# Four kinds of attention in one kernel: the sums of a wide step in a ring of four PSUM banks, and a query's low part first

## The reference, cut to what matters

```
q, k, v = x @ Wq, ctx @ Wk, ctx @ Wv          # layers 0, 2: heads of 64
logits  = q k^T * scale + col_bias            # -20 * (1 - mask) on chosen keys
x       = softmax(logits) @ v @ Wo + bo + x
xn      = x * rsqrt(mean(x*x) + eps) * norm_w # layers 1, 3: heads of 16
x       = x + softmax(q k^T * scale) @ v @ wo
```

## Time and profile before

| | |
|---|---|
| median of 3 runs | 1754.18 us (1751.69 to 1755.21) |
| the profiled execution's own time | 1748.67 us |
| its span (first to last instruction) | 1746.9 us |
| PE / DVE / ACT / POOL busy | 93% / 69% / 59% / 27% of the span |
| chain that ended last | PE 46%, issue 16%, DVE 10%, POOL 7%, ACT 3% |
| granted TensorE clock, mean | 0.968 |

### The profile page before, as it was taken

The page is one execution under the profiler, slowest core; times in us unless marked ns, Lnnn a source line. Parts: engine busy times, 40 slices in busy tenths (PEclk is TensorE's granted clock), DMA queues, the critical chain, the costliest instruction groups (busy, mean ns, idle before and its releaser), DMA issues.

```text
span 1746.9 us, 29686 instructions
## 1 busy us (share of the span) xinstructions
PE 1617.9 (93%) x10732; PEld 882.6 (51%) x10732; DVE 1197.9 (69%) x2313; ACT 1023.9 (59%) x1737; POOL 471.9 (27%) x353
## 2 busy tenths in 40 slices
PE   7998698999999999999999999899999999999794
PEld 6886444444545454544545454445454545454442
DVE  5474547676777687768777777678777877775551
ACT  2111165666667676767666766576676767676452
POOL 5342402123222231223131313132322322232212
PEclk9898898999999999999999999999999999999986
DMA  7998402151315121512353323412151325131422
GB/s 255 323 317 242 140 25 58 37 98 28 84 32 132 27 78 27 131 35 80 69 115 91 73 54 80 91 40 72 41 122 27 82 41 125 26 81 23 123 69 81
DMA packets 176738, 160.57 MB, mean 92 GB/s; under 512 B 91722, under 2 KB 133066, under 8 KB 175570
## 3 DMA queue, kind: packets, MB, share of 16 engines
q1 hardware_dynamic: 174578, 150.29, 33.5%
q10 hardware_dynamic: 2016, 8.39, 1.2%
HBM read 115.11 MB, written 43.48 MB: 91 GB/s over the span
## 4 chain that ended last, share of the span: by engine, by line
PE 46%; issue 16%; DVE 10%; POOL 7%; ACT 3%; SPq 3%; DMA 3%; POOLq 0%; ACTq 0%; DVEq 0%
PE general L1649 9%; PE general L1528 7%; POOL kept L1402 4%; PE score_ps L1587 4%; PE score_ps L1588 4%; PE out_ps L1605 4%; PE general L1545 3%; PE general L1549 3%; PE score_ps L1576 2%; PE out_ps L1625 2%; DVE q_pair L1440 2%; DVE q_aux L1439 2%; SPq L1135 2%; DVE q_pair L1441 2%; PE general L1669 2%
## 5 line engine op out<-in xcount | busy, mean ns | idle before, releaser
L1451 DVE TENSOR_REDUCE tops<-general 128x2 bf16<-128x308 f32 x1024 | 433.2, 470 | 88.1 <-PE general L1545 40.1
L1292 ACT ACTIVATE probs<-score_ps 128x512 f32<-128x512 f32 x512 | 297.7, 598 | 141.0 <-PE score_ps L1588 128.0
L1402 POOL TENSOR_TENSOR kept<-kept,inv_b 128x512 f32<-128x512 f32 x128 | 170.7, 1355 | 464.9 <-DMA inv_b<-scratch_inverses 464.9
L1438 DVE CAST q_aux<-q_pair 64x512 bf16<-64x512 f32 x160 | 74.8, 468 | 194.1 <-ACT q_pair L1280 192.9
L1304 ACT ACTIVATE q_aux<-general 4x512 bf16<-4x512 bf16 x320 | 187.5, 586 | 31.7 <-PE general L1558 26.1
L1279 ACT ACTIVATE q_pair<-general 64x512 fp32r<-64x512 f32 x160 | 94.6, 591 | 156.7 <-PE general L1528 156.1
L1545 PE MATMUL general<-w_top,q_aux 128*128 128x154 bf16 x1024 | 133.4, 237 | 36.5 <-DVE q_pair L1441 26.1
L1341 ACT ACTIVATE a_hi<-kept 128x512 fp32r<-128x512 f32 x160 | 93.6, 624 | 112.0 <-POOL kept L1402 48.1
L1464 DVE TENSOR_TENSOR a_lo<-kept,a_hi 128x512 fp32r<-128x512 f32 x160 | 123.9, 807 | 49.7 <-ACT a_hi L1341 48.9
L1392 POOL TENSOR_TENSOR x_lo<-xn,x_hi 128x1024 fp32r<-128x1024 f32 x31 | 73.6, 2375 | 285.0 <-ACT x_hi L1260 145.6
L1588 PE MATMUL score_ps<-q_pair,w_pair 128*128 128x512 f32 x256 | 149.4, 589 | 0.0
(11 more groups left out here) (157 smaller groups left out, 3305.7 us busy)
## 6 DMA issues: line engine op xcount, KB each, us to landing
inv_b<-scratch_inverses SPq DMA_DIRECT2D x128, 256.0 KB, 4.8
w_pair<-scratch_wk_hi SPq DMA_DIRECT2D x32, 256.0 KB, 4.9
x<-scratch_stream SPq DMA_DIRECT2D x16, 512.0 KB, 3.3
inv_n<-scratch_inverses SPq DMA_DIRECT2D x256, 32.0 KB, 1.9
xn<-scratch_stream SPq DMA_DIRECT2D x15, 512.0 KB, 3.4
scratch_stream<-x SPq DMA_DIRECT2D x14, 512.0 KB, 4.9
scratch_wk_hi<-p_kout_hi SPq DMA_DIRECT2D x16, 308.0 KB
p_raw<-in_L_xattn_Wk_dram SPq DMA_DIRECT2D x4, 1024.0 KB, 7.8
```

The lines of the kernel that those rows point to most:

```text
L1292: nc.scalar.activation(dst, score_ps[:, number % 2, :], ACT.Exp, scale=scale).then_inc(act_exp.sem, 1)
L1402: last = nc.gpsimd.tensor_tensor(tiles[i], tiles[i], (inv_b, inv_n)[n % 2][:, i, :], ALU.mult)
L1451: last = nc.vector.tensor_reduce(tops[:, n % 2, sub, 2 * pair:2 * pair + 2], src, AX_X, ALU.max)
```

## The change

1. `GB` is 4. sum_ps is gone; value n 1 of a wide step takes a bank of the ring for its sums, with `start=True` at every step. DVE takes the bank: at the first step of a chunk as a copy to wide_sums, at the three others as an addition to it. ACT's copy and PE's wait for it are gone.
2. DVE does a query's two subtractions before its two casts.
3. `ORDER`, `FIRST` and `LAST` are new throughout. In `FIRST` query 8 0 and 8 1 come in step 2.
4. At the start of the layers POOL, not DVE, clears the first half of q_aux, and ACT, not SP, issues the DMAs of w_top's key rows and of the first mask rows.
5. In `prepare` both layers' norm weights are loaded behind the second piece of weights.

```
-        normw = sb("p_normw", [P, KC])
+        normw = sb("p_normw", [P, 2, KC])
...
                 load_piece(1)
+                for p in range(2):
+                    sp.dma_start(normw[:, p, :], ins[f"L{2 * p + 1}_xattn_norm_w"].rearrange("(k p) -> p k", p=P)).then_inc(s_nw, 16)
...
-GB = 3
+GB = 4
...
-GENERAL = [(*x, m) for x in PLAN if x[1] in ("query", "max", "turn", "output", "square", "rate", "give")
+WIDE_STEPS = [n for n in range(STEPS) if wide(n)]
+GENERAL = [(*x, m) for x in PLAN if x[1] == "value" and x[2] in WIDE_STEPS and x[3] == 1 or x[1] in ("query", "max", "turn", "output", "square", "rate", "give")
...
-        sum_ps = ctx.enter_context(nc.psum_tensor("sum_ps", [P, 512], F32))
...
-        reader = {"query": dve_query, "max": dve_max, "turn": act_turn, "output": dve_output,
+        reader = {"value": dve_sums, "query": dve_query, "max": dve_max, "turn": act_turn, "output": dve_output,
...
         def _(act):
+            act.wait_ge(rows_cleared, 1)
+            load_top_rows(act, 0)
+            act.wait_ge(first_cleared, 1)
+            load_masks(act, 0)
...
-                elif what == "sums":
-
-                    if n % 2 == 0:
-                        wait(act, pe_value.sem, pe_value.after(it, "value", 4 * n + 3, 1))
-                        wait(act, sums_stored.sem, sums_stored.after(it - (n == 0), what, 2 - n, 0))
-                        nc.scalar.activation(wide_sums[:], sum_ps[:], ACT.Copy).then_inc(act_sums.sem, 1)
...
         def _(pool):
+            nc.gpsimd.memset(q_aux[:, 0].bitcast(F32), 0.0).then_inc(first_cleared, 1)
...
-            for buf in (w_top[:], q_aux[:, 0], w_aux[:], w_aux_rest[:], tops[:]):
+            for buf in (w_top[:], w_aux[:], w_aux_rest[:], tops[:]):
...
-                    nc.vector.tensor_copy(q_aux[0:64, t, s, j, :], q_pair[0:64, s, j, :])
-                    nc.vector.tensor_copy(q_aux[64:P, t, s, j + 1, :], q_pair[64:P, s, j + 1, :]).then_inc(dve_aux.sem, 1)
                     nc.vector.tensor_tensor(q_pair[64:P, s, j, :], ps[0:64], q_pair[0:64, s, j, :], ALU.subtract)
                     last = nc.vector.tensor_tensor(q_pair[0:64, s, j + 1, :], ps[64:P], q_pair[64:P, s, j + 1, :], ALU.subtract)
                     last.then_inc(dve_query.sem, 1)
+                    nc.vector.tensor_copy(q_aux[0:64, t, s, j, :], q_pair[0:64, s, j, :])
+                    nc.vector.tensor_copy(q_aux[64:P, t, s, j + 1, :], q_pair[64:P, s, j + 1, :]).then_inc(dve_aux.sem, 1)
...
+                elif what == "value":
+
+                    if not wide(n) or k == 0:
+                        return
+                    wait(dve, pe_value.sem, pe_value.after(it, what, n, k))
+                    ps = bank_of((it, what, n, k, 0))
+                    if n % 4 == 0:
+                        wait(dve, sums_stored.sem, sums_stored.after(it - (n == 0), "sums", 2 - n // 4, 0))
+                        nc.vector.tensor_copy(wide_sums[:], ps).then_inc(dve_sums.sem, 1)
+                    else:
+                        wait(dve, dve_sums.sem, dve_sums.after(it, what, n - 1, 1))
+                        nc.vector.tensor_tensor(wide_sums[:], ps, wide_sums[:], ALU.add).then_inc(dve_sums.sem, 1)
...
                         if k == 1:
+                            sum_ps = bank((it, what, n, k, 0))
                             for j in range(4):
                                 nc.tensor.matmul(sum_ps[SUMS[j]], sel[:, g, :], probs[:, j, :],
-                                                 start=(g == 0), stop=False, skip_group_check=True)
+                                                 start=True, stop=False, skip_group_check=True)
```

Two lines of `ORDER` as an example, step 9 to 10 of each window:

```
-        max 10 3, value 9 0, max 10 4, max 10 5, square 3, score 9 3, max 10 6, max 10 7, query 11 0,
-        query 11 1, turn 10, value 9 1, rate 3, inverse 1, max 11 0, max 11 1,
+        squares 3, score 9 2, max 10 6, max 10 7, score 9 3, query 11 0, square 3, query 11 1, turn 10,
+        value 9 0, value 9 1, rate 3, max 11 0, max 11 1, max 11 2,
```

More of the change, by code:

```diff
@@ L573 @@
 ORDER = """
[L574 to L585, removed]
@@ new lines @@
+    rest 1, max 2 0, low 2- 3, value 0 1, max 2 1, max 2 2, score 1 0, inverse 3-, output 2- 3, max 2 3,
+        score 1 1, max 2 4, score 1 2, max 2 5, max 2 6, squares 1, max 2 7, score 1 3, query 3 0,
+        square 1, query 3 1, scale 3- 0, turn 2, value 1 0, value 1 1, rate 1, max 3 0,
+    rest 2, max 3 1, max 3 2, max 3 3, score 2 0, max 3 4, score 2 1, max 3 5, early 2, max 3 6, score 2 2,
+        max 3 7, score 2 3, query 4 0, turn 3, value 2 0, value 2 1, max 4 0, max 4 1, max 4 2,
@@ new lines @@
+    rest 0, score 0 0, max 1 0, max 1 1, score 0 1, max 1 2, max 1 3, scale 2- 2, scale 2- 3, max 1 4,
+        score 0 2, norm 2- 2, max 1 5, value 0 0, sums 3-, max 1 6, max 1 7, score 0 3, low 2- 2,
+        query 2 0, query 2 1, turn 1, value 0 1, output 2- 2, norm 2- 3,
+    rest 1, low 2- 3, max 2 0, score 1 0, max 2 1, score 1 1, max 2 2, score 1 2, output 2- 3, max 2 3,
+        max 2 4, score 1 3, value 1 0, max 2 5, squares 1, max 2 6, max 2 7, query 3 0, square 1,
+        query 3 1, turn 2, value 1 1, rate 1,
@@ new lines @@
+    rest 10, max 11 2, max 11 3, max 11 4, score 10 0, nkeys 0 2, score 10 1, nkeys 0 3, rate 3, max 11 5,
+        max 11 6, score 10 2, value 10 0, score 10 3, max 11 7, turn 11, value 10 1, low 1 0,
+    rest 11, score 11 0, query 12 0, score 11 1, score 11 2, output 1 0, score 11 3, value 11 0, scale 1 1,
+        value 11 1, max 12 0, max 12 1, sums 2, max 12 2, max 12 3, norm 1 1, max 12 4, max 12 5, max 12 6,
+        max 12 7, inverse 2, turn 12, low 1 1, scale 2 0, query 14 0, max 13 0,
@@ L846, in __init__ @@
         for w, what, n, k in PLAN:
-            if what in kinds and n in only:
+            if what in kinds and n in only and k in parts:
                 made += times
@@ L1597, in do @@
                         pe.wait_ge(filled, 1)
-                    if n in (0, 8) and k == 0:
-                        wait(pe, act_sums.sem, act_sums.after(it - (n == 0), "sums", 2 - n // 4, 0))
                     rest = probs_rest[:, n % 4, :]
```

370 lines of the change are left out of this document (179 added, 191 removed).

## The result

The changed kernel takes 1727.78 us (median of 4 runs, 1724.81 to 1728.54) against 1752.93 for the kernel before. The ratio worked out over all runs is 0.9874, with a 95% interval of 0.9849 to 0.9898: 22 us, where the two medians by themselves lie 25 us apart. A second set of runs gave 0.9874 again (0.9853 to 0.9895). The forecast was 1712 in a range of 1692 to 1742: the sign and the range hold, but the gain is 22 us where I had 42.

What follows compares the result with a forecast made beforehand. PE (TensorE), busy 1617.9 of 1746.9 us, was taken to bound the kernel. The terms -34 - 4 + 6 - 2 - 6 - 2 = -42 us, taken from the median 1754.18, gave 1712 us, range 1692 to 1742.

Steps and rivals of the forecast that it cites:

- Query banks: PE's waits for ring banks released by DVE's low part of a query, 39.1 us: 34 us of them go.
- Low first: Subtractions before casts free a query's bank 0.84 us earlier; casts come 1.4 us later, covered by turn and value, costed at nothing.
- Max banks: PE's waits for banks released by max reductions, 5.7 us: 4 us of them go.
- Additions on the path: DVE's 64 copies and additions of the sums, 44.2 us: 6 us of it on the path, bounds 0 and 44.2.
- New lists: Reordering beyond the first window: 6 us gained of 17.2 us of waits for probs, a_lo and scores, bounds 0 and 17.2.
- First window: Query 8 0 and 8 1 in step 2 remove PE's wait of 2.18 us for query 8 0's cast: 2 us gained.
- windows, 178.5 us: A repeating window of the layers was to take about 178.5 us instead of 183.3.
- Start: At the start of the layers, POOL's clearing and ACT's DMAs bring first max and first reduction earlier: 2 us gained.
- The end: The last chunk's sums go through the same chain of steps as before: 0 us.
- Rival one: DVE is late where fullest, in step 8: half the additions' time on the path, half the query waits stay; 1745 us, chance 0.14.
- Rival three: PE meets the next limit at once, ACT's rows and exponentials; half of the gain stays; 1733 us, chance 0.14.
- Rival two: The sums' bank makes the ring one of three again; bank waits stay, additions delay PE at 64 steps; 1797 us, chance 0.07.

Runs made afterwards that it cites:

- run 9: The changed kernel with the old lists and casts first, so the ring of four with the sums in it and the new start remain: 1740.83 us, 0.9946.
- run 5: The changed kernel again, unedited: 1730.00 us, 0.9874 to the kernel before.
- run 11: The changed kernel with a query's two casts before its two subtractions again, measured a second time: 1721.67 us, 0.9848 to the kernel before.
- run 6: The changed kernel with the 48 additions of the sums cut to 8 columns and the inverse replaced by a copy: 1723.71 us, 0.9838 to the kernel before.
- run 7: The changed kernel with each of the 48 additions done twice, the extra one into a spare tile: 1741.10 us, 0.9941 to the kernel before.
- run 4: The kernel before with the new lists alone (ring of three, own bank of sums, casts first): 1843.23 us, 1.0528.
- run 1: The changed kernel with a query's two casts before its two subtractions again, first measurement: 1722.55 us, 0.9845 to the kernel before.
- run 3: The changed kernel with the old ORDER, FIRST and LAST: 1756.06 us, 1.0025 to the kernel before.

## Why the prediction was right, and nearly twice too large

**Query banks, -34: the size and the reason are wrong.** The waits did go in the trace, from 39.1 us to under 2. But "a bank is asked for again one use later" holds only where no sums lie between, and they lie between a query and the next maxima at just the places that wait; the timeline of run 9 shows the same 0.77 us with a fourth bank. The ring with its additions is worth 9.4 us (0.0054 x 1750). With the cost of the additions put back (some 11 us, an estimate worked out below), the bank itself is worth some 20.

**Low first, part of the -34, price "nothing": this is the step that failed.** It costs 7.6 us in the old kernel (medians), 14 with the old lists in the new ring, and likely 4.9 in the change. I named the cover (turn and value lie between a query and its max) and stopped at the max that waits for the cast. It shows in the list all the same, 9.0 + 5.1 us against 2.2, none of it between 560 and 1500 us. The longest, 4.4 us, is the very first max, which waited as long for the masks before. And I counted a wait that goes as time gained, though another DVE operation stood a few instructions behind it: the reductions, the product and x. The price had a second part, the casts themselves. The groups of the two casts, whole run (busy us, mean ns), in the kernel before 74.8 + 90.2 = 165.0 us in all, in low first alone, same number and size, 24.9 us more:

```profile
L1442 DVE CAST q_aux<-q_pair 64x512 bf16<-64x512 f32 x160 | 97.3, 608 | 2.1
L1441 DVE CAST q_aux<-q_pair 64x512 bf16<-64x512 f32 x160 | 92.6, 579 | 4.9
```

In the changed kernel they take 86.2 + 99.2 = 185.4 us, in run 5 the same kernel has 179.2, and with casts first in the new lists they take 172.2 (run 11). So with the new lists low first lengthens them by 7 to 13 us, and the rest of their growth goes with the ring and lists. It is also why DVE is at 1250.8 us and not at my 1242: 20.4 us more of casts, less 5.9 of reductions and some 6 of others.

**Max banks, -4: wrong sign in the list.** Waits for the reductions rose from some 8 us to 20 in all. That is where part of the query waits went.

**Additions on the path, +6: the place right, the size probably low.** My 6 stood for all 44.2 us of copies and additions. Run 6 gains 6.3 us for 25.2 of them, run 7 loses 11.1 for 33 more. At run 6's slope the whole would cost 11 us, an estimate. The changed kernel at the place that I read:

```profile
1022.34 0.65 PE L1680 MATMUL general<-ident,rate 128*128 128x128 f32 x4
...
1022.56 0.69 DVE L1458 TENSOR_TENSOR wide_sums<-general,wide_sums 128x512 f32<-128x512 f32 x1 [0.75 <-PE general L1623]
...
1022.83 0.79 PE L1551 MATMUL general<-w_top,q_aux 128*128 128x154 bf16 x6
...
1023.30 0.11 PEld L1551 LDWEIGHTS general<-w_top,q_aux 128*128 128x128 bf16 x2 [0.24 <-DVE wide_sums L1458]
```

From the rate to max 11 0 it takes 0.49 us instead of 1.42. The weights of the third max wait 0.24 us for the addition, which ends at 1023.25: nearly "just in time".

**New lists, -6: far too small.** On top of the ring of four, with casts first, they give 0.9946 - 0.9847 = 0.0099, or 17 us, the very end of the bounds (17.2), which I had set by waits for ACT and a_lo. Those waits didn't fall, they rose, so that the size meets the bound is chance. What the lists do is to make the fourth bank pay: with casts first the two rows of the low part stand at 12.7 us in the new order (run 11) and at 30.6 in the old (run 9). At the place of rows 6 the wait of max 11 0 went by the order alone. In run 4, the kernel before with the new lists, it starts 0.49 us behind the rate without waiting, and the next limit stands right behind it:

```profile
1107.27 0.65 PE L1673 MATMUL general<-ident,rate 128*128 128x128 f32 x4
1107.76 0.43 PE L1542 MATMUL general<-w_top,q_aux 128*128 128x154 bf16 x4
1109.30 0.31 PE L1542 MATMUL general<-w_top,q_aux 128*128 128x154 bf16 x2 [1.11 <-DVE xn L1492]
```

With a ring of four and casts first (run 11) it is 0.49 us again. The mean-square step stands between the two queries now, and DVE's waits for its matmuls fell from 20.1 us in 16 (run 9) to 5.9 in 4 (run 11). I had seen both there, the order and the bank, and booked them under the bank. Taken together, ring and lists with the first window, were booked at -34 - 4 + 6 - 2 - 6 = -40 and gave -27.

**First window, -2: far too small as well; windows, 178.5 us: too good.** By the stretches, in us, from single profiles (granted clock of the first stretch and of the rest behind them):

| | first stretch | five windows | rest | clock |
|---|---|---|---|---|
| before | 387.4 | 917.2 | 249.6 | 0.96, 0.91 |
| ring of four alone (run 9) | 386.1 | 914.7 | 248.6 | 0.96, 0.92 |
| casts first (run 1) | 383.8 | 900.6 | 253.8 | 0.95, 0.90 |
| casts first (run 11) | 372.8 | 903.3 | 250.3 | 0.97, 0.90 |
| the change | 371.9 | 905.2 | 253.9 | 0.97, 0.89 |
| the change (run 5) | 374.2 | 909.9 | 253.3 | 0.96, 0.91 |

Two profiles of one kernel differ by up to 11 us in the first stretch and 4.8 in the five windows. From run 9 to run 11 the new lists give 13.3 us in the first stretch, where I had read one place (to run 1 it is 2.3, at the lower clock), and 11.4 in five windows. A window of the change is 2.4 us shorter (1.5 in run 5), not the 4.8 that I had; my own working, 32 us over seven windows, would have made it 4.6. The earlier trace rows also began a window too early: the step at 397.81 still belongs to the list of the beginning.

**Start, -2; norm weights, 0.** From the first query matmul to the first reduction it is 9.77 us (191.65 to 201.42) instead of 10.85 (192.77 to 203.62), so 1.1 for my 2. The first max stands at 199.03, under 200 as forecast, but for another reason: the layers began 1.1 us earlier, and this beginning differs by 7 us between the profiles of all these kernels (188.8 to 196.1), which is the preparation's own scatter. What came in place of the late masks:

```profile
198.55 0.42 DVE L1436 CAST q_aux<-q_pair 64x512 bf16<-64x512 f32 x1
```

PE's wait of 4.49 us for the masks is one of 4.4 us for this cast, which now ends at 198.97; I had it at 199.2 to 199.5. Counted from the first query matmul, the first max comes 0.08 us earlier (7.38 against 7.46 us): what the masks gave, the cast took. For the norm weights ACT had waited 20.9 us in two waits; now it waits 20.1 us in two for the weights themselves, so 0 is right.

**The end, 0:** 4.3 us were given back there. With casts first it is 0.7 in one profile and 4.2 in the other (the table), and the granted clock is 0.89 to 0.91 in the kernels with new lists against 0.91 and 0.92 with the old, so whether casts, lists or clock cost it stays open.

**The sum as measured:** ring with additions -9.4, lists -17.3, low first +4.9: -22 us, with the start inside the first. The parts depend on the order in which they are added: with low first already in, the lists give 26 us (run 3 against the change). That the range holds owes something to luck: had the lists given only the 8 us booked for them and the first window, the same sum on the forecast's own base would stand at 1741 to 1742 us, at the range's very end.

**The rivals.** Rival one (DVE late where it is fullest, 1745) is out as written: additions cost a quarter to a third of their time, not half. Rival three (the next limit at once, half of the gain stays, 1733) is nearest to the measured time. Its waits for ACT did rise, from 12.2 to 21.8 us in all, as one of my signs of being wrong had it. The waits for DVE's casts and reductions rose more, from 10 to 34 us, and no run makes ACT faster or slower, so its part in the missing 20 us isn't measured. Rival two is out; in a ring that truly is one of three the kernel takes 1803 us, for its 1797, but that run has the new lists and the rival was priced from the old ones, so the two figures meet by chance. The Trainium skill's advice to mind PSUM pressure ("Trainium Kernel Development and Optimization", Best Practices) does not decide here with four banks. With three, where PE waits for banks that DVE has yet to empty, the same kernel takes 73 us more.

## What to carry to other kernels

A wait that heads the list is worth what stands behind it leaves: before booking it, follow the engine that releases it to its next customers, since an earlier release by a reordered queue moves the wait and doesn't remove it. A bank added to a ring counts only at places where no new use was added between, so count uses at the places that wait, in the new order. Take more than one profile before a difference of a few us is read from a stretch. And order and buffers can't be priced apart: the same lists cost 5% with three banks and gain 1% with four, the same exchange of two operations saves 74 us where banks are scarce and costs some 5 to 14 where they aren't.

## What the runs showed of the hardware

A cast from SBUF to SBUF on VectorE takes longer beside an operation of GpSimd. In low first alone:

```profile
983.70 0.68 DVE L1438 TENSOR_TENSOR q_pair<-general,q_pair 64x512 fp32r<-64x512 f32 x1 [1.63 <-ACT q_pair L1280]
984.39 2.70 POOL L1402 TENSOR_TENSOR kept<-kept,inv_n 128x512 f32<-128x512 f32 x2 [5.10 <-DMA inv_n<-scratch_inverses]
984.39 0.69 DVE L1439 TENSOR_TENSOR q_pair<-general,q_pair 64x512 fp32r<-64x512 f32 x1
985.12 0.83 DVE L1441 CAST q_aux<-q_pair 64x512 bf16<-64x512 f32 x1
985.96 1.41 DVE L1442 CAST q_aux<-q_pair 64x512 bf16<-64x512 f32 x1
```

The casts take 0.83 and 1.41 us instead of 0.42, beside two POOL operations of 1.35 us each that end at about 985.74 and 987.09; the subtraction that reads a bank takes its 0.69 us beside the same operations. In the kernel before 36 of the 320 casts took over 0.6 us, in low first alone 60, in the change 58, and every one of them overlaps a POOL operation. Between 21 and 26 others in each overlap one by over 0.1 us and stay short. The subtractions lie between 683 and 696 ns in all of them. The low part a_lo, a subtraction with both inputs in SBUF, behaves as the casts do: 0.63 us at the least, 0.69 at the median, 1.78 at the most in the kernel before, where all 22 over 0.8 us overlap a POOL operation. Low first puts casts 1.4 us later, and that is more often beside POOL's scaling. The Trainium skill says so in general ("GPSIMD Engine Reference", Specifications: the SBUF interfaces are shared with VectorE, with contention for its instructions in a 2-port mode or with two SBUF inputs). The trace agrees for a_lo, which has two; in which mode the casts run it doesn't tell. It adds the size: the longest cast took 2.36 us for 0.42, nearly all others stay under 1.53, and all casts together take 165.0 us before, 185.4 in the change, 189.9 in low first alone. I had the spread of 0.40 to 1.45 us in the earlier trace rows before me and read it only as a bank held longer; it also meant that casts have a better and a worse moment. That the stretched casts alone cost the 7.6 us wasn't tried; a kernel with POOL's scaling held back would tell.
